# A two-layer recurrent-attention kernel: the second projections of layer 1 are issued as 64 units inside the full attention

## The reference, cut to what matters

```python
A_hidden = A.transpose(0, 2, 1, 3).reshape(b, s, H)
qa = (A_hidden @ Wqa.T + bqa).reshape(b, s, NH, HD).transpose(0, 2, 1, 3)
ka = (A_hidden @ Wka.T + bka).reshape(b, s, NH, HD).transpose(0, 2, 1, 3)
g = jnp.einsum('bhqd,bhkd->bhqk', qa, ka) * SCALE
g = jnp.where(causal[None, None], g, -jnp.inf)
pg = jax.nn.softmax(g, axis=-1)
out = jnp.einsum('bhqk,bhkd->bhqd', pg, A)
out = out.transpose(0, 2, 1, 3).reshape(b, s, H)
return out @ Wd.T + bd
```

## Time and profile before

| what | us |
| --- | --- |
| median of 3 runs | 2437.94 |
| lowest and highest | 2432.04, 2554.12 |
| the profiled execution | 2441.48 |
| its span (core 5, the slowest) | 2439.9 |
| spans of the eight cores | 2418.9 to 2439.9 |
| PE, DVE, ACT busy in the span | 1694.4, 1416.3, 1246.2 |

### The profile page before, as it was taken

How to read it: one execution, slowest core, us unless ns; L and a number is a source line. 1 busy time by engine, 2 the same in 40 slices (tenths; PEclk the granted TensorE clock), 3 DMA queues, 4 the chain that set the end, 5 groups by cost and what they waited for, 6 DMA issues and landing times.

```text
span 2439.9 us, 23103 instructions; the slowest of 8 cores (2418.9 to 2439.9 us)
## 1 busy us (share of the span) xinstructions
PE 1694.4 (69%) x7431; PEld 649.6 (27%) x7431; DVE 1416.3 (58%) x1689; ACT 1246.2 (51%) x1353; POOL 262.3 (11%) x276
## 2 busy tenths in 40 slices
PE   0157367776666775529999987986679947777774
PEld 0012122222222221214444432332553312122221
DVE  8787598988568988223332026145642386655442
ACT  1583388898678887311111123123445434668771
POOL 1000043333110000210000000000120000010001
PEclk9978676777666666859999999998559957899997
DMA  7552310111251100473220021011121120010001
GB/s 163 113 103 40 56 26 14 25 22 24 77 115 20 26 1 1 125 145 70 52 52 26 1 48 22 1 18 18 31 48 31 26 44 35 35 52 18 35 36 60
DMA packets 103694, 113.23 MB, mean 46 GB/s; under 512 B 80148, under 2 KB 80564, under 8 KB 101496
## 3 DMA queue, kind: packets, MB, share of 16 engines
q1 hardware_dynamic: 91192, 71.05, 11.3%
q0 software_dynamic: 12384, 40.69, 10.3%
HBM read 115.96 MB, written 16.81 MB: 54 GB/s over the span
## 4 chain that ended last, share of the span: by engine, by line
PE 41%; DVE 23%; ACT 17%; issue 12%; DMA 4%; POOL 1%; SPq 1%; DVEq 0%; ACTq 0%; POOLq 0%
PE PS L1338 9%; PE PS L1446 5%; PE PS L1379 5%; DVE cs L926 4%; ACT pt L1750 4%; PE PS L1776 3%; PE PS L1552 2%; PE PS L1811 2%; PE PS L790 2%; DVE rf L1786 2%; PE PS L1735 2%; DMA xres<-x 2%; DVE rt L1468 2%; PE PS L1485 2%; PE PS L821 2%
## 5 line engine op out<-in xcount | busy, mean ns | idle before, releaser
L1750 ACT ACTIVATE pt<-PS,negb 128x1024 bf16<-128x1024 f32 (+2 forms) x240 | 228.0, 1023 | 149.0 <-PE PS L1735 149.0
L1338 PE MATMUL PS<-xn_fm,wgu 128*128 128x512 bf16 x1024 | 223.7, 382 | 0.0
L956 PE MATMUL PS<-sq,bones 128*128 128x512 bf16 x256 | 101.3, 539 | 166.7 <-ACT sq L939 166.7
L1491 DVE TENSOR_REDUCE mx<-PS 16x1 f32<-16x1024 f32 x64 | 77.6, 1212 | 175.1 <-PE PS L1485 175.1
L790 PE MATMUL PS<-xn_fm,wz 128*128 128x512 bf16 x512 | 141.3, 439 | 29.4 <-SPq L111 26.3
L926 DVE TENSOR_TENSOR_SCAN cs<-vr,carr 128x1024 bf16<-128x1024 bf16 x64 | 148.9, 2368 | 0.0
L1348 ACT ACTIVATE rl<-PS 128x1024 bf16<-128x1024 f32 x32 | 32.8, 1024 | 224.2 <-PE PS L1338 218.3
L926 DVE TENSOR_TENSOR_SCAN cs<-vr 128x1024 bf16<-128x1024 bf16 x64 | 142.9, 2273 | 0.0
L1338 PEld LDWEIGHTS PS<-xn_fm,wgu 128*128 128x128 bf16 x1024 | 100.7, 98 | 122.5 <-issue 3.4
L939 ACT ACTIVATE sq<-cs 128x1024 bf16<-128x1024 bf16 x128 | 127.8, 1047 | 7.7 <-DVE cs L926 6.0
L1735 PE MATMUL PS<-RK,RV 64*128 64x512 bf16 (+3 forms) x640 | 96.5, 381 | 47.8 <-ACT pt L1750 45.3
(11 more groups left out here) (261 smaller groups left out, 3269.9 us busy)
## 6 DMA issues: line engine op xcount, KB each, us to landing
wz<-l_wz POOLq DMA_DIRECT2D x32, 384.0 KB, 5.4
xt<-x SPq DMA_DIRECT2D x8, 1024.0 KB, 7.0
xres<-x SPq DMA_DIRECT2D x16, 512.0 KB, 4.5
...
```

The source lines that it names most:

```text
L956: t = do("tensor", lambda e, _s=s2, _r=r: e.matmul(PM[:, _s * 512:(_s + 1) * 512], bones[:], sq[_r][k][:, _s * 512:(_s + 1) * 512], start= ...
L1338: g = (lambda e, _w=w, _f=f, _d=dc, _b=bb, _t=tt: e.matmul(PS[:, _b + _f * 512:_b + (_f + 1) * 512], _w[:, _d * 512 + _f * 128:_d * 512 + ...
L1750: e.activation(pt[_g][:, 0:_o], PS[:, _b:_b + _o], AF.Exp, bias=sb["negb2"][:, _h:_h + 1], scale=0.125))
```

## The change

- The barrier, `project` for the second projections, and the one bound over all heads are gone. The projections are 64 **units** of 512 tokens: 8 matmuls into half of a ring slot; DVE adds the bias and writes bf16 (it was ACT); ACT squares 512 columns after the exponentials of the same step; in the next unit PE multiplies the squares by a block matrix `hb` into the other half of that unit's slot, and DVE takes the maximum.
- Units go pair by pair: 4 for the keys and 4 for the queries of a pair. Ten are issued ahead, then one in front of each step of the attention (steps 0 to 53), so that a pair is ready before its first step.
- The bound is made per pair (`bound_1`, `bound_2`): two small DVE maxima, a product, Ln, Exp, a scaling, then a matmul against ones and a copy. `bound_2` takes a ring slot.
- The steps have another order: block 3 of all pairs first (64 steps), then per pair block 2 and block 0 (8 steps), then block 1 (32 steps).
- The output is in half tiles (9 matmuls each, half a slot), 24 of them in front of steps 72 to 158, 8 after the last step. Residual and result have two buffers each, which lie in the upper part of RQ; Wd is loaded into the lower part after the last unit.
- The finished outputs go into RK in place of the queries. `pt` has 5 buffers for 4.

The diff, without allocations, the old body of `dense` (printed above), and the memory views:

```diff
+    def chunk(n):
+        return n if n < 16 else 16 + (n - 16) // 2 + 8 * (n % 2 == 0)
...
-    need("tensor", *t_af, t_n[47], t_n[46])
-    st["z"] = [t_e[46], t_e[47]]
-    for oc in range(16, 32):
-        project(oc, lambda o: RQ[:, o:o + 512], RK if oc < 24 else RV,
-                16 * ((oc - 16) // 8), False)
-    settle_late()
-    t_b2 = bound(0, sb["negb2"])
-    kb.barrier()
...
-    NP = 4
-    pt = [kb.S(f"pt{i}", (128, 1024), BF16)[:] for i in range(3)]
+    NP = 5
...
+    yio = RQ[:, 8192:16384].bitcast(F32)
+    xo = [yio[:, i * 2048:i * 2048 + 1024] for i in two]
+    yo = [yio[:, i * 2048 + 1024:i * 2048 + 2048] for i in two]
...
+    old = [t_e[46], t_e[47], t_m[46], t_m[47], t_pv[46], t_pv[47], t_n[46], t_n[47],
+           *t_af]
+    need("vector", *old)
+    need("scalar", *old)
...
-        need("tensor", t_x.get(k - NB))
+        if k >= NB:
+            need("tensor", *t_x[k - NB])
...
+    def unit(u):
+        p, j = divmod(u, 8)
+        n = 16 + u // 4
+        k, base = buf()
+        if u < 64:
+            w = wp[n % NW]
+            need("tensor", t_wp[n])
+            for dc in range(8):
+                f = (lambda e, _d=dc: e.matmul(
+                    PS[:, base:base + 512], w[:, _d * 128:(_d + 1) * 128],
+                    RQ[:, _d * T + (u % 4) * 512:_d * T + (u % 4 + 1) * 512],
+                    start=(_d == 0), stop=(_d == 7)))
+                t = do("tensor", f) if dc == 7 else kb.op("tensor", f)
+            if u % 4 == 3 and n + NW < 32:
+                t_wp[n + NW] = load_wp(n + NW, t)
+            t_unit[0] = t
+            dst = (KA if j < 4 else QA)[:, p * T + (u % 4) * 512:
+                                        p * T + (u % 4 + 1) * 512]
+            need("vector", t)
+            t_ev[u] = do("vector", lambda e: e.tensor_scalar(
+                out=dst, in0=PS[:, base:base + 512],
+                scalar1=sb["bproj"][:, chunk(n):chunk(n) + 1], scalar2=None,
+                op0=ALU.add))
+            t_x[k] = (t_ev[u],)
+            unit_sq.append((u, dst))
+        if u > 0:
+            need("tensor", t_s2[u - 1])
+            t_nm[u - 1] = t = do("tensor", lambda e: e.matmul(
+                PS[:, base + 512:base + 1024], hb[:], sq2[(u - 1) % 2][:],
+                start=True, stop=True))
+            need("vector", t, t_nb1.get((u - 1) // 8 - 2))
+            c = ((u - 1) // 8 % 2) * 8 + (u - 1) % 8
+            t_red[u - 1] = do("vector", lambda e: e.tensor_reduce(
+                nmx[:, c:c + 1], PS[:, base + 512:base + 1024], AX.X, ALU.max))
+            t_x[k] = (t_red[u - 1],)
...
+    def settle_square():
+        while unit_sq:
+            u, dst = unit_sq.pop()
+            need("scalar", t_ev[u], t_nm.get(u - 2))
+            t_s2[u] = do("scalar", lambda e: e.activation(
+                sq2[u % 2][:], dst, AF.Square, bias=0.0, scale=1.0))
...
+    def bound_1(p):
+        c = (p % 2) * 8
+        need("vector", t_red[8 * p + 7])
+        for k in two:
+            v = do("vector", lambda e, _k=k: e.tensor_reduce(
+                nbt[:, _k:_k + 1], nmx[:, c + 4 * _k:c + 4 * _k + 4], AX.X, ALU.max))
+        t_nb1[p] = v
+        need("vector", v)
+        v = do("vector", lambda e: e.tensor_tensor(
+            nbt[:, 2:3], nbt[:, 0:1], nbt[:, 1:2], ALU.mult))
+        need("scalar", v)
+        a = do("scalar", lambda e: e.activation(nbt[:, 3:4], nbt[:, 2:3], AF.Ln,
+                                                bias=0.0, scale=1.0))
+        need("scalar", a)
+        a = do("scalar", lambda e: e.activation(nbt[:, 4:5], nbt[:, 3:4], AF.Exp,
+                                                bias=0.0, scale=0.5))
+        need("vector", a)
+        t_nb[p] = do("vector", lambda e: e.tensor_scalar(
+            out=nbt[:, 6:8], in0=half2[:], scalar1=nbt[:, 4:5],
+            scalar2=-0.125 / 64.0, op0=ALU.mult, op1=ALU.mult))
...
+    def bound_2(p):
+        k, base = buf()
+        need("tensor", t_nb[p])
+        t = do("tensor", lambda e: e.matmul(PS[:, base:base + 2], onesf,
+                                            nbt[:, 6:8], start=True, stop=True))
+        need("vector", t)
+        v = do("vector", lambda e: e.tensor_copy(
+            sb["negb2"][:, 2 * p:2 * p + 2], PS[:, base:base + 2]))
+        t_x[k] = (v,)
+        t_b2[p] = v
...
+        need("tensor", t_ev[8 * p + 7])
...
-            need("scalar", t if r else t_even, t_pt[g])
...
+            need("scalar", t_sc[r], t_pt[g], t_b2[p])
...
-                need("vector", v, t_wdm.get(b - 2))
-                t_fin[(b, p)] = do("vector", lambda e: e.tensor_tensor(
-                    ofm[b % 2][:, p * 512:(p + 1) * 512], nf[q][:], rf[q][:],
+                need("vector", v)
+                t_fin[(b, p)] = t_nf[q] = do("vector", lambda e: e.tensor_tensor(
+                    QA[:, p * T + b * 512:p * T + (b + 1) * 512], nf[q][:], rf[q][:],
                     ALU.mult))
...
-    def dense(i):
+    t_y, t_o, t_x1 = {}, {}, {}
+    order_y = []
+    def dense(i, s):
         b, c = i // 4, i % 4
-        need("sync", t_y.get(i - 1))
-        t_x1 = dma("sync", "s_xo", lambda e: e.dma_start(out=xo[:],
-                                                              in_=x1v[i]))
+        if s == 0:
+            order_y.append(i)
+        n = len(order_y) - 1
+        y, x = yo[n % 2], xo[n % 2]
+        prev = order_y[n - 2] if n > 1 else None
+        if s == 0:
+            need("sync", t_y.get(prev), t_unit[0])
+            t_x1[i] = dma("sync", f"s_xo{n % 2}", lambda e: e.dma_start(
+                out=x, in_=x1v[i]))
         k, base = buf()
...
+        need("tensor", t_fin[(b, 7)], t_wdT[0])
+        o = PS[:, base:base + 512]
+        kb.op("tensor", lambda e: e.matmul(
+            o, sb["ones64b"][:], sb["bdh"][:, s * 512:(s + 1) * 512],
+            start=True, stop=False))
+        for p in range(8):
+            a = p * T + b * 512 + c * 128
+            f = (lambda e, _p=p, _a=a: e.matmul(
+                o, QA[:, _a:_a + 128],
+                wdT[:, _p * 1024 + s * 512:_p * 1024 + (s + 1) * 512],
+                start=False, stop=(_p == 7)))
+            t = do("tensor", f) if p == 7 else kb.op("tensor", f)
...
+        need("vector", t, t_o.get(prev))
+        if n < 2:
+            need("vector", t_unit[0])
+        t_x[k] = (do("vector", lambda e: e.tensor_tensor(
+            y[:, s * 512:(s + 1) * 512], o,
+            G[:, i * D + s * 512:i * D + (s + 1) * 512], ALU.mult)),)
+        if s == 1:
+            need("gpsimd", t_x[k][0], t_x1[i])
+            t_y[i] = do("gpsimd", lambda e: e.tensor_tensor(y, y, x, ALU.add))
+            need("sync", t_y[i])
+            t_o[i] = dma("sync", f"s_out{n % 2}", lambda e: e.dma_start(
+                out=outv[i], in_=y))
...
+    t_wdT = [None]
+    for u in range(10):
+        unit(u)
+        settle_square()
+        if u == 8:
+            bound_1(0)
+        if u == 9:
+            bound_2(0)
+    steps = [(p, 3, k2) for p in range(8) for k2 in range(8)]
+    steps += [(p, b, k2) for p in range(8) for b in (2, 0) for k2 in range(2 * b + 2)]
+    steps += [(p, 1, k2) for p in range(8) for k2 in range(4)]
+    halves = {72 + 7 * j: (12 + j // 2, j % 2) for j in range(8)}
+    halves.update({130 + 15 * j // 8: (8 * (j < 8) + j // 2 % 4, j % 2)
+                   for j in range(16)})
     held = []
-    for b in range(4):
-        for p in range(8):
-            for k2 in range(2 * b + 2):
-                fresh = scores(p, b, k2)
-                for args in held:
-                    weigh(*args)
-                held = fresh
-            if b > 0 and p in (1, 2, 3, 4):
-                dense(4 * (b - 1) + p - 1)
+    for s, (p, b, k2) in enumerate(steps):
+        u = s + 10
+        if u <= 64:
+            unit(u)
+        if u == 64:
+            need("gpsimd", t_unit[0])
+            t_wdT[0] = dma("gpsimd", "s_wdT", lambda e: e.dma_start(
+                out=wdT, in_=H["l1_wdT"][:, :]))
+        if s in halves:
+            dense(*halves[s])
+        fresh = scores(p, b, k2)
+        settle_square()
+        if u % 8 == 0 and u <= 64:
+            bound_1(u // 8 - 1)
+        if u % 8 == 1 and 8 < u <= 65:
+            bound_2(u // 8 - 1)
+        for args in held:
+            weigh(*args)
+        held = fresh
     for args in held:
         weigh(*args)
-    for i in range(12, 16):
-        dense(i)
-    need("sync", t_o[15])
+    done = set(halves.values())
+    for i in (0, 1, 2, 3, 4, 5, 6, 7):
+        for s in two:
+            if (i, s) not in done:
+                dense(i, s)
+    need("sync", *[t_o[i] for i in order_y[-2:]])
```

100 lines of the change are left out of this document (46 added, 54 removed).

## The result

The changed kernel took **2507.4 us**, median of 4 runs (2492.2 to 2551.4), against 2438.2 for the kernel before: a ratio of **1.027, 95% interval 1.023 to 1.031**. The forecast was 2412; it is **slower**, and outside the range. In one of the four runs one half of the chip (four of its cores) was slower throughout and in another in part, so I compare stages by the profiled execution (2492.2 us, span 2490.5) and take 2492 to 2497 as the time of the changed kernel, 54 to 59 us above the kernel before (these two runs alone would give a ratio of 1.023).

A forecast was written before the change was run, and what follows sets the result against it. Different limits by stage: PE in the projections, ACT in block 3, DVE in block 0, DMA and POOL at the end. Terms 25.5 + 251 + 186 + 92 + 45 = 599.5 for 625.8 us gave 2412 us, range 2355 to 2450.

The forecast's parts named there:

- The ten units ahead: Before the attention: ten units of 2.05 us, plus 5 us for clock, memsets and bound, sum 25.5 us.
- the end: After the last step: finish, two halves, product, then tiles every 6.9 us behind SP's residual load, sum 45 us.
- the durations of bias, maximum and square: Block 3, operations of 512 columns: bias near 0.69 us, maximum 0.7 on DVE, square 0.63 on ACT.
- the stall behind the finish: Block 3: PE waits 4.6 us per finish for DVE's bias and maximum queued behind it, 28 us for six pairs.
- the finishes of blocks 2 and 0: Interleaved blocks 2 and 0: the two finishes of one pair stand 8 us apart.
- The first rival: Block 3: DVE's stall does not reach PE and the norm never waits; 50 us less, 2362 us; chance 0.25 with partial forms.
- pair with units: Block 3: 28.5 us per pair at 3.65 per step, plus 4.6 stall and about 1 us wait for the bound.
- blocks 2 and 0: Interleaved stage: 22 us per pair, plus 10 us in all for eight half tiles, sum 186 us.
- block 1: PE's 4.1 us lie beside the finish, DVE's two products do not: 11.5: Block 1: 10.0 us per pair plus two halves, only DVE's products of 0.69 paid; 11.5 x 8 = 92 us.
- a chain over PE and ACT: Block 3 step with a unit: scores, exponentials, square, norm in sequence, 3.65 us, against 3.48 of PE's own work.
- the clock falls: Rival: half clock from the first pairs of blocks 2 and 0 to block 1's end, +100 us, 2512; chance 0.06.
- The rival at 2512: Blocks 2, 0 and 1 at half clock, +6 and +6.5 us per pair, 100 us in all; chance 0.06.

The follow-up runs named there:

- run without tiles: Changed kernel with block 1's 16 half tiles moved behind the last step: 2497.0 us, ratio 1.025 to the kernel before.
- the finish in pieces and the addition on DVE: Changed kernel with reciprocal and product in four pieces, next residual loaded before the store, residual addition moved from POOL to DVE: 2419.5 us, ratio 0.995.
- pieces alone: Changed kernel with the finish's reciprocal and product in four pieces of 128 columns, one per step, behind the unit's bias and maximum: 2440.1 us, ratio 1.002.

## Why the prediction was wrong

**What held.** The ten units ahead; the end; the durations of bias, maximum and square; the stall behind the finish, its place and its size (4.41 for 4.6); the finishes of blocks 2 and 0, 8.1 apart in six of eight pairs; block 1 without tiles (9.9 for 10.0). The first rival (no stall) did not occur. That the ends of the sum fit within 1 us does not make the middle right: all of the miss lies in three terms.

**The step that failed: the price of what stands in DVE's queue, in stages where PE, ACT and DVE pass work in a ring.** The terms "pair with units", "blocks 2 and 0" and above all **"block 1: PE's 4.1 us lie beside the finish, DVE's two products do not: 11.5"** were mis-sized. Per pair they measured 37.4 to 39.9 us for 34.1 (the pair and its waits), 25.5 for 23.3, and 16.0 for 11.5.

*Block 1, +36.* I took PE's 4.1 us for two halves as hidden beside the finish and paid only DVE's two products. The run without tiles shows 6.1 us per pair for two halves. The overlap was not there: with the finish in pieces and the addition on DVE two halves still cost 4.1 us per pair, PE's whole time, for ACT waits while PE works at the half (4.0 to 5.9 of ACT idle before the exponentials behind ten of them, which I had counted for whole tiles and not here). The other 2 us are DVE's queue and POOL: the product behind the finish that keeps the slot (2.62 in the rows; pieces alone give 1.3 per pair) and the masks behind POOL's addition (1.5 per pair without additions), which in part stand in for each other. What the lower clock costs the halves is in all of these and was not measured alone.

*Block 3, +27.* Per pair 3.2 us: 0.8 of steps at 3.79 for 3.65, 1.1 where pairs meet (the slot of the bound), 1.35 at half rate behind the stall. Seven pairs make 22, and two of them were 1.6 and 2.5 longer. The step itself was near its forecast for a reason that I had wrong: I called it a chain over PE and ACT with PE at 3.48, but with the norm's wait taken away it stays at 3.69 with PE all but fully busy. So the overlap that the first rival counted on, steps at 3.48, was not there to be had either.

*Blocks 2 and 0, +18.* From the second pair on pairs were 24.8 to 27.4 apart where 22 and 1.3 for tiles were forecast. The order on DVE was as forecast; but the granted clock was 0.76 there, where I expected above 0.85, and in 12 us windows it went between 0.51 and 1.00, so matmuls took the time of both levels. I had this as a price of the rival "the clock falls", but not in my own sum. That the clock is the cause of the 18 us is an argument from the rows, and no run tests it alone: the finish in pieces brings this part down to 188.7 at the same clock (0.75).

**The rival at 2512** named nearly the time, but not the cause: it wanted half the clock through both stages. The rows show 0.76 and 0.85, so that it came near the measured time is chance. Half rate came in stretches behind waits of PE; what it cost in all was not measured alone. The forecast's remark that block 0 of the kernel before agreed with a swing between the two levels was too strong: it stood at 0.50 throughout. The swing shows in the changed kernel. With the finish in pieces the clock of block 3 is 0.96 for 0.93.

**POOL against DVE** was in no rival, though every number for it was there: additions of 2.34 us on POOL and 192 masks on DVE in the same stages. Before, they did not meet: each of the 12 additions inside the attention ran beside the four PSUM copies of a finish, which kept their 0.69 us, and none beside a mask. In the changed kernel ten of these 12 meet masks. The Trainium skill ("SBUF — State Buffer", "Who interferes with whom") says that a DVE instruction with two inputs in SBUF and a GpSimd instruction that reads SBUF contend for a shared port pair, and that whichever starts first keeps it for its whole instruction while the other blocks. The trace agrees: a mask started 0.06 us behind an addition ends 0.09 us after it, at 2.37 us for 0.21, and without additions on POOL the masks' mean is 222 ns.

**Why interleaving lost.** It puts PE work beside ACT's exponentials, but with a unit in it the step is PE's, so only 0.18 us per unit are hidden. Against that a unit brings DVE two operations and a ring slot in every step, and the finish of 7 us in one lump holds that slot. With the units ahead of the attention the same finish holds nothing that PE needs at once: pairs of block 3 then follow at 16.2 us, the pace of the exponentials. With the lump cut, the same overlap gains 7 us of the 10.
